# Four SSM states weighted by one GpSimd instruction, norm shifts on VectorE, and a new work order

## The reference

```
xn  = layernorm(x) * (1 + scale) + shift
u   = silu(conv(xn @ W_in));  dt = softplus(u @ W_x[:, :64] @ W_dt + b);  B, C = u @ W_x[:, 64:]
h_n(t) = h_n(t-1) * exp(dt(t) * A_n) + dt(t) * u(t) * B_n(t)       # per channel, all t in order
y(t)   = sum_n h_n(t) * C_n(t)
out = x + gate * ((y + u * D) * silu(z)) @ W_out
```

## Time and profile before

| | |
|---|---|
| median of 3 runs | 2023.14 us (2008.57 to 3804.73) |
| profiled execution | 2021.5 us, span 2019.3 us |
| busy: TensorE / VectorE / ScalarE / GpSimd | 1817.7 / 1780.9 / 1710.2 / 1789.5 us (90 / 88 / 85 / 89% of the span) |
| mean granted clock of TensorE | 0.961 |
| weightings on GpSimd (L969) | 510, 1197.2 us in all |
| scans on VectorE (L1581, L1578) | 576 + 448, 1198.5 us in all |
| DMA | 302.29 MB, mean 150 GB/s |

### The profile page before, as it was taken

The page is one execution under the profiler, slowest core; times in us unless marked ns, Lnnn a source line. Parts: engine busy times, 40 slices in busy tenths (PEclk is TensorE's granted clock), DMA queues, the critical chain, the costliest instruction groups (busy, mean ns, idle before and its releaser), DMA issues. The chain is left out here.

```text
span 2019.3 us, 29111 instructions
## 1 busy us (share of the span) xinstructions
PE 1817.7 (90%) x9252; PEld 1265.7 (63%) x9252; DVE 1780.9 (88%) x1818; ACT 1710.2 (85%) x3224; POOL 1789.5 (89%) x823
## 2 busy tenths in 40 slices
PE   8979688998989999998999999898998999697778
PEld 7555555757667575766667575656757575455666
DVE  5458999889999999999989999999989999898983
ACT  2488788989989999999989999999989998777662
POOL 0059999999999999999999999999999999999970
PEclk8989699999999999999999999999999999898999
DMA  7034554444445545454444545445444545454430
GB/s 279 1 110 156 169 165 149 139 159 155 150 140 171 167 146 181 130 182 153 146 150 152 178 149 175 147 157 162 157 140 155 166 154 180 142 162 142 155 105 11
DMA packets 163784, 302.29 MB, mean 150 GB/s; under 512 B 18904, under 2 KB 27312, under 8 KB 162096
## 3 DMA queue, kind: packets, MB, share of 16 engines
q1 hardware_dynamic: 153110, 287.45, 43.9%
q10 hardware_dynamic: 10522, 12.99, 2.1%
HBM read 292.98 MB, written 5.29 MB: 148 GB/s over the span
## 5 line engine op out<-in xcount | busy, mean ns | idle before, releaser
L969 POOL TENSOR_TENSOR state<-state,c_rows 128x1024 f32<-128x1024 f32 x510 | 1197.2, 2382 | 26.3 <-DVE state L1578 13.6
L1581 DVE TENSOR_TENSOR_SCAN state<-decay,mix_banks 128x512 f32<-128x512 f32 x576 | 673.1, 1206 | 15.7 <-ACT decay L1303 0.7
L2016 PE MATMUL bank<-const_sb,state 128*128 128x128 f32 x4096 | 546.4, 281 | 38.1 <-POOL state L969 37.7
L2016 PEld LDWEIGHTS bank<-const_sb,state 128*128 128x128 f32 x4096 | 482.1, 145 | 145.9 <-issue 76.4
L1578 DVE TENSOR_TENSOR_SCAN state<-mix_banks,state 128x512 f32<-128x512 f32 x448 | 525.4, 1204 | 48.0 <-ACT mix_banks L1284 36.4
L960 POOL TENSOR_TENSOR state<-kept,b_rows 128x1024 f32<-128x1024 f32 x224 | 532.4, 2381 | 19.7 <-DMA b_rows<-flat_rows 10.3
L1303 ACT ACTIVATE decay<-kept,ssm_pack 128x512 f32<-128x512 f32 x576 | 395.2, 716 | 17.0 <-DVE state L1581 14.2
L1571 DVE TENSOR_TENSOR mix_banks<-kept,mix_banks 128x1024 f32<-128x1024 f32 x288 | 353.5, 1227 | 42.4 <-ACT mix_banks L1292 33.6
L1284 ACT ACTIVATE mix_banks<-kept,ssm_pack 128x512 f32<-128x512 f32 x448 | 302.0, 683 | 57.4 <-DVE state L1581 42.2
L1836 PE MATMUL bank<-kept,conv_diag 128*128 128x512 f32 x496 | 225.3, 597 | 4.3 <-ACT kept L1224 3.8
L987 ACT ACT_TABLE_LOAD x165 | 211.7, 1283 | 8.8 <-issue 5.8
(11 more groups left out here) (206 smaller groups left out, 2237.9 us busy)
## 6 DMA issues: line engine op xcount, KB each, us to landing
b_rows<-flat_rows SPq DMA_DIRECT2D x512, 256.0 KB, 3.9
c_rows<-flat_rows SPq DMA_DIRECT2D x512, 256.0 KB, 3.6
conv_diag<-conv_diag SPq DMA_DIRECT2D x8, 1024.0 KB, 7.3
out<-x_res ACTq DMA_DIRECT2D x8, 512.0 KB, 3.2
ssm_pack<-ssm_pack SPq DMA_DIRECT2D x2, 1907.0 KB, 12.4
x_next<-x ACTq DMA_DIRECT2D x6, 512.0 KB, 6.7
x_again<-x_dbl ACTq DMA_DIRECT2D x16, 128.0 KB, 4.3
state<-ada_w SPq DMA_DIRECT2D x1, 1536.0 KB, 14.3
```

What stands on the lines that cost most here:

```text
L969: pool.tensor_tensor(st, st, by_pair(c_rows[:, row % ROWS]), ALU.mult).then_inc(m_prod, 1)
L1581: ins = dve.tensor_tensor_scan(st, decay[:, nth(g) % DECAYS], mixed, 0.0, ALU.mult, ALU.add)
L2016: ins = pe.matmul(y_banks[c2][:, t * P:(t + 1) * P], state[:, g % STATES, t * P:(t + 1) * P], ident, start=False, stop=(g == BANK_SUMS[g / ...
```

## The change

- **Weighting.** `weight` multiplies four states (two pairs, units g to g+3 with g a multiple of 4) by their two C rows in one GpSimd instruction over 128 x 2048, once both rows are loaded and scan g+3 is done. 510 instructions become 255. `m_prod` counts fours, so the sums, the C rows and ScalarE's `dtr` step wait for multiples of four. The two late pairs stay.
- **State slots.** 14 become 16 (a group of four always starts at a multiple of 4).
- **Shifts.** The 48 `shift` instructions move from GpSimd to VectorE, at the stages `root` and `yroot` of the tables, in front of `normed` where VectorE does the norm.
- **C rows.** SyncE issues C row g-3 behind B row g, where it was g-1, and the wait for a free C slot is rounded up to whole fours. At the end of a scan three C rows follow the last B row.
- **Order.** All the tables are new except the last attention's, which moves by a step in two places. Counted over the whole tables, in quarters of a unit: the weighting stands on average 6.0 behind the place of its last scan before and 3.7 after; the inject of a BESIDE pair stands 13.7 behind the sum that frees its slot before and 9.9 after; it leads its scan by 15.2 before and 17.3 after.

```diff
-BANKS, DECAYS, STATES, ROWS = 3, 7, 14, 4
+BANKS, DECAYS, STATES, ROWS = 3, 7, 16, 4
+WEIGHED = 4
...
-FIRST_BASES = {'att': (-53, -28), 'setup': -49, 'prep': -33}
-TAIL_BASE, POST_BASE, PREP_BASE = -19, -50, 8
-ATT_BASES, LATE_BASES = (18, 100, 153, 222), (41, 193)
+FIRST_BASES = {'att': (-53, -28), 'setup': -48, 'prep': -33}
+TAIL_BASE, POST_BASE, PREP_BASE = -17, -40, 9
+ATT_BASES, LATE_BASES = (17, 100, 152, 219), (51, 193)
...
+C_BEHIND = 3
...
-    "weight": (11, 7, 10, 5, 9, 8, 6, 8, 9, 14, 14, 11, 15, 13, 12, 8, 7, 8, 12, 7, 5, 8, 6, 12, 11, 19, 17, 14,
...
+    "weight": (25, 15, 16, 18, 16, 16, 15, 15, 17, 15, 13, 20, 19, 17, 17, 19, 15, 20, 13, 20, 19, 17, 17, 20, 19,
...
-    "weight": range(0, ALL_UNITS - HC * LATE_PAIRS, HC),
+    "weight": range(0, ALL_UNITS - HC * LATE_PAIRS, WEIGHED),
...
-                for g in range(HALVES * N + 1):
+                for g in range(HALVES * N + C_BEHIND):
...
-                    if g > 0:
-                        slot, n = (g - 1) % ROWS, (g - 1) % N
-                        past(sp, m_prod, si * HALVES * N + g - ROWS)
+                    if g >= C_BEHIND:
+                        g -= C_BEHIND
+                        slot, n = g % ROWS, g % N
+                        past(sp, m_prod, ((si * HALVES * N + g + 1 - ROWS) * HC + WEIGHED - 1) // WEIGHED)
...
-            def shift(norm, root, done, k):
-                pool.wait_ge(root, k)
-                pool.tensor_tensor(norm["shift"][:, :, 0], norm["minus"][:, :, 0], norm["rstd"][:, :, 0],
-                                   ALU.mult).then_inc(done, 1)
...
             def weight(g):
                 si, half, n, c2, c = split(g)
-                row = half * N + n
-                pool.wait_ge(c_loaded[row % ROWS], 16 * (si * (HALVES * N // ROWS) + row // ROWS + 1))
-                pool.wait_ge(m_scan, g + HC)
-                st = pair_states(g)
-                pool.tensor_tensor(st, st, by_pair(c_rows[:, row % ROWS]), ALU.mult).then_inc(m_prod, 1)
+                row, pairs = half * N + n, WEIGHED // HC
+                for k in range(row, row + pairs):
+                    pool.wait_ge(c_loaded[k % ROWS], 16 * (si * (HALVES * N // ROWS) + k // ROWS + 1))
+                pool.wait_ge(m_scan, g + WEIGHED)
+                st = state[:, g % STATES:g % STATES + WEIGHED, :].rearrange("p (n c) t -> p n c t", c=HC)
+                by_row = c_rows[:, row % ROWS:row % ROWS + pairs, :].unsqueeze(2).broadcast_to([P, pairs, HC, T])
+                pool.tensor_tensor(st, st, by_row, ALU.mult).then_inc(m_prod, 1)
...
-                past(act, m_prod, (pi - 1) * UNITS // HC)
+                past(act, m_prod, (pi - 1) * UNITS // WEIGHED)
...
+            def shift(norm, root, done, k):
+                dve.wait_ge(root, k)
+                dve.tensor_tensor(norm["shift"][:, :, 0], norm["minus"][:, :, 0], norm["rstd"][:, :, 0],
+                                  ALU.mult).then_inc(done, 1)
...
+                yield from w.to("root")
+                shift(att_norm, a_root, a_rstd, 2 * ai + 1)
                 yield from w.to("xn")
...
+                yield from w.to("yroot")
+                shift(att_norm, a_root, a_rstd, 2 * ai + 2)
+                if (ai, 1) in VECTOR_NORMS:
                     yield from w.to("yn")
...
+                yield from w.to("root")
+                shift(prep_norm, p_root, p_rstd, pi + 1)
+                if pi in VECTOR_PREPS:
                     yield from w.to("xn")
...
-                    pe.wait_ge(m_prod, g // HC + 1)
+                    pe.wait_ge(m_prod, g // WEIGHED + 1)
```

More of the change, by code:

```diff
@@ L198 @@
-    2: (199, 199, 210, 213, 215, 217, 219, 218, 218, 218, 224, 230, 231, 237, 240, 246, 251, 254, 257, 265, 269,
-        273, 276),
-    3: (216, 216, 218, 218, 219, 221, 222, 224, 224, 224, 226, 228, 230, 232, 237, 239, 245, 251, 253, 255, 258,
-        264, 266),
-    4: (201, 201, 206, 211, 216, 215, 217, 216, 216, 216, 218, 219, 219, 221, 228, 234, 237, 240, 240, 240, 240,
-        240, 240),
-    5: (213, 213, 216, 216, 218, 217, 221, 220, 220, 220, 224, 222, 227, 229, 234, 238, 240, 242, 242, 242, 242,
-        242, 242),
@@ L206 @@
-    6: (203, 203, 206, 210, 215, 220, 221, 222, 222, 222, 224, 227, 231, 233, 245, 251, 254, 261, 265, 268, 271,
-        274, 274),
-    7: (213, 213, 216, 216, 218, 219, 223, 222, 222, 222, 226, 225, 228, 230, 237, 240, 246, 253, 255, 260, 264,
-        267, 274),
-    8: (201, 201, 210, 213, 214, 215, 217, 216, 216, 216, 218, 218, 220, 222, 228, 234, 237, 240, 240, 240, 240,
-        240, 240),
-    9: (204, 204, 206, 212, 216, 217, 219, 218, 218, 218, 220, 219, 223, 225, 231, 236, 239, 246, 246, 246, 246,
-        246, 246),
@@ L214 @@
-    10: (201, 201, 206, 213, 218, 219, 225, 220, 220, 220, 231, 231, 236, 237, 243, 249, 253, 260, 265, 269, 270,
-         273, 276),
-    11: (215, 215, 218, 218, 220, 220, 224, 223, 223, 223, 225, 226, 227, 229, 236, 239, 243, 252, 254, 258, 264,
-         269, 272),
-    12: (200, 200, 202, 211, 214, 216, 217, 217, 217, 217, 218, 218, 219, 221, 227, 233, 237, 240, 240, 240, 240,
-         240, 240),
-    13: (204, 204, 210, 212, 213, 215, 216, 219, 219, 219, 220, 220, 222, 225, 230, 236, 238, 246, 246, 246, 246,
-         246, 246),
@@ L222 @@
-    14: (202, 202, 210, 211, 212, 215, 216, 218, 218, 218, 218, 218, 219, 220, 226, 229, 231, 230, 237, 239, 245,
-         252, 254),
-    15: (3, 3, 144, 144, 145, 147, 147, 154, 172, 206, 207, 207, 208, 210, 213, 213, 217, 214, 217, 221, 224, 224,
-         225),
+    0: (156, 156, 158, 159, 160, 173, 174, 180, 180, 180, 184, 182, 188, 190, 196, 199, 204, 206, 206, 206, 206,
+        206, 206),
+    1: (160, 160, 174, 176, 177, 178, 179, 179, 179, 179, 180, 181, 182, 185, 191, 197, 200, 206, 206, 206, 206,
+        206, 206),
@@ new lines @@
+    2: (173, 173, 176, 179, 180, 181, 191, 190, 190, 190, 194, 193, 196, 197, 200, 206, 212, 215, 221, 230, 234,
+        238, 242),
+    3: (180, 180, 182, 183, 184, 184, 186, 186, 186, 186, 188, 191, 195, 196, 199, 204, 210, 213, 229, 231, 234,
+        238, 242),
+    4: (167, 167, 174, 174, 175, 175, 176, 175, 175, 175, 177, 176, 178, 179, 184, 190, 196, 198, 198, 198, 198,
+        198, 198),
+    5: (164, 164, 170, 174, 176, 177, 177, 178, 178, 178, 178, 179, 179, 181, 190, 196, 198, 202, 202, 202, 202,
+        202, 202),
@@ new lines @@
+    6: (165, 165, 170, 176, 178, 181, 185, 186, 186, 186, 187, 188, 189, 192, 197, 199, 205, 211, 217, 222, 227,
+        231, 234),
+    7: (175, 175, 182, 183, 186, 185, 193, 189, 189, 189, 196, 195, 197, 198, 202, 208, 213, 215, 226, 230, 233,
+        238, 246),
+    8: (161, 161, 166, 173, 174, 175, 175, 175, 175, 175, 176, 177, 177, 179, 184, 190, 196, 198, 198, 198, 198,
+        198, 198),
+    9: (167, 167, 170, 174, 176, 177, 178, 178, 178, 178, 179, 181, 183, 185, 194, 197, 203, 206, 206, 206, 206,
+        206, 206),
@@ new lines @@
+    10: (170, 170, 174, 175, 180, 178, 187, 186, 186, 186, 190, 190, 192, 194, 198, 203, 208, 212, 218, 224, 229,
+         233, 238),
+    11: (174, 174, 177, 179, 179, 179, 186, 182, 182, 182, 188, 188, 192, 195, 199, 205, 210, 213, 219, 224, 228,
+         233, 238),
+    12: (165, 165, 170, 173, 174, 175, 175, 175, 175, 175, 176, 177, 177, 178, 183, 189, 196, 198, 198, 198, 198,
+         198, 198),
+    13: (164, 164, 166, 169, 173, 179, 181, 183, 183, 183, 184, 185, 188, 190, 196, 199, 204, 206, 206, 206, 206,
+         206, 206),
@@ L226 @@
+    14: (163, 163, 166, 172, 178, 181, 182, 183, 183, 183, 184, 184, 187, 189, 197, 201, 207, 206, 214, 217, 223,
+         228, 230),
+    15: (2, 2, 87, 96, 99, 100, 101, 110, 129, 166, 167, 167, 168, 170, 173, 173, 177, 174, 177, 181, 184, 184, 185),
 })
 TAIL_STAGES = by_name(TAIL_NAMES, {
-    0: (104, 105, 106, 106, 109),
-    1: (2, 68, 72, 73, 75),
-    2: (61, 75, 78, 86, 91),
-    3: (59, 73, 77, 85, 91),
-    4: (73, 88, 91, 93, 95),
-    5: (62, 75, 77, 79, 86),
-    6: (61, 75, 76, 79, 88),
@@ L235 @@
-    7: (61, 75, 77, 80, 92),
-    8: (74, 88, 89, 90, 94),
-    9: (63, 75, 77, 81, 89),
-    10: (62, 75, 77, 81, 90),
-    11: (62, 75, 76, 84, 91),
-    12: (69, 88, 90, 91, 94),
-    13: (62, 75, 76, 77, 89),
-    14: (56, 75, 80, 83, 89),
-    15: (59, 74, 77, 82, 87),
+    0: (94, 97, 98, 98, 103),
+    1: (3, 60, 64, 65, 67),
+    2: (50, 65, 66, 82, 85),
+    3: (50, 66, 70, 80, 86),
+    4: (68, 82, 85, 86, 90),
+    5: (63, 65, 67, 80, 82),
+    6: (61, 66, 67, 79, 83),
+    7: (51, 67, 72, 79, 85),
@@ L244 @@
+    8: (67, 81, 84, 85, 90),
+    9: (60, 66, 71, 77, 81),
+    10: (54, 68, 73, 78, 82),
+    11: (50, 66, 71, 77, 84),
+    12: (72, 81, 82, 83, 85),
+    13: (62, 66, 72, 78, 81),
+    14: (50, 67, 72, 75, 84),
+    15: (50, 66, 70, 83, 87),
 })
-SETUP_STAGES = dict(zip(SETUP_NAMES, (2, 47, 25, 51, 62, 96, 80, 84, 121, 147, 73, 168, 176, 179), strict=True))
+SETUP_STAGES = dict(zip(SETUP_NAMES, (0, 44, 22, 52, 74, 92, 77, 80, 117, 143, 69, 164, 172, 175), strict=True))
```

(30 more changed lines are left out.)

4 lines of the change are left out of this document (removed), and 414 rows, old and new, of tables (ATT_STAGES, PREP_STAGES, STEPS).

## The result

The changed kernel takes 2082.81 us (median of 4 runs, 2072.38 to 2086.02) against 2020.12 us for the kernel before: a ratio of 1.0321, 95% interval [1.0256, 1.0386]. It is 3.2% slower, where 1.5% faster was forecast. The ratio goes by the fast runs alone, so it leaves out a run of the kernel before of 3804.73 us. The profiled execution took 0.8 us less than its median (2081.98 us, span 2079.8 us).

A forecast was written before the change was run, and what follows sets the result against it. GpSimd, busy for 96.6% of the loop, was taken as the tightest engine, with VectorE next. The terms -36 - 6 - 8 + 1 + 18 = -31 us gave 1992 us against the median, range 1983 to 2005.

The forecast's parts named there:

- What one instruction of four states saves: GpSimd's weightings: one of 4.50 us replaces two of 2.32 us, 0.14 us saved for each of 255, 36 us.
- The price of a shift on VectorE: The 42 shifts in the loop: 0.18 us each on VectorE, 8 us, from a row before the loop.
- Which lie in VectorE's idle time of 1846.4 - 1704.2 = 142 us: VectorE in the loop: its idle time of 142 us covers the 8 us of shifts moved there.
- Rival 3: Loop's shifts on VectorE wait for GpSimd's instruction, 1.8 us on the mean; 2027 to 2145 us, centre 2040; chance 0.16.
- It decides from 1.7 us a shift on: VectorE in the loop: shift waits set the time once they reach 1.7 us each.
- Its counter-argument: VectorE's PSUM bank waits: a stall lets ScalarE fill banks, so part of it replaces 70 us of waits.
- The cited rule: VectorE instructions with two SBUF inputs and GpSimd ones reading SBUF contend; whichever starts second is blocked until the first ends.
- Slots, rows and order: GpSimd's waits before weightings and injects: thinner cushions add 18 us; C rows and slots 0, order 0 with 15 either way.
- The move off GpSimd: 42 shifts leaving GpSimd's queue in the loop: 6 us of work and 8 us of waits saved.
- Its signs of being wrong as a whole: The loop moving by more than 60 us either way, or the ends (111 and 62 us) by more than 3.

The follow-up runs named there:

- e2: Changed kernel with each shift on VectorE as four one-column instructions, rstd as scalar operand, so one SBUF tensor is read; 1994.23 us, ratio 0.9917.
- r5: Changed kernel with one-column shifts on VectorE and two states to a weighting instead of four; 1999.43 us, ratio 0.9938.
- e1: Changed kernel with the 48 shifts back on GpSimd at the same stages of the new tables; 2044.64 us, ratio 1.0166.
- r10: Kernel before with one-column shifts on VectorE and 16 state slots in place of 14, old tables and pairs; 2029.25 us, ratio 1.0079.
- e4: Kernel before with only the 48 shifts moved to VectorE, each as four one-column instructions; 2023.42 us, ratio 1.0061.
- r8: Changed kernel with one-column shifts on VectorE, each issued twice, once into a spare tile; 2015.56 us, ratio 1.0018.

## Why the prediction was wrong

- **What one instruction of four states saves: right.** 4.49 us from start to start (4.50), and 1742.8 us of GpSimd in the loop (1742). What it was worth is another matter: against pairs in the same tables, 4 us (e2 against r5).
- **The price of a shift on VectorE: the step that failed.** "For the forecast I take the low end, as it is the only row of this shape": 0.18 us, from a stretch in which GpSimd was idle. The loop has GpSimd busy for 91 to 97%, and there a shift took 107.0 / 42 = 2.55 us (all but the six outside, of 0.16 us each). The nearest row by shape was the farthest by condition.
- **"Which lie in VectorE's idle time of 1846.4 - 1704.2 = 142 us": wrong, and the larger error of method.** 81 us of stalls cost 81 us, 44 cost 46, and 23 us of plain work cost 20. Much of VectorE's idle time is made of short waits in front of scans and products for PSUM banks (70 us in all), and a stall elsewhere in its queue doesn't fill them; this reading fits the three doses but was not tested by itself. GpSimd, the busiest engine by share at 96.6%, did not set the time alone: 34 us less of its work brought 4, at the price of 26 us more of waits for scans.
- **Rival 3 is what happened, in mechanism and place; its sizes were short.** It gave 2040 as its centre and a chance of 0.16. It asked for 1.8 us of waiting on the mean, by a shift that comes at any time; a shift of 2.55 us was measured. Two things make the difference. 4 waits passed over further instructions. And shifts don't come at any time: of the 23 that began inside a weighting, 16 had more than 3.3 of its 4.5 us before them, 3.15 on the mean where 2.25 was put. From the measured 2.55 us its own sum makes (1704 + 107) / 0.966 = 1875 us of loop, and 1910.6 were measured: VectorE was busy for 1805.8 us, about as it says, but only for 94.5% of the loop. "It decides from 1.7 us a shift on" sets VectorE against GpSimd's old 1784 us; against the 1742 us that GpSimd would have left it is from (1742 - 1704) / 42 = 0.9 us on. The 65.5 us that ScalarE waited for the shift, and the chain behind it, had been left out; they are where to look for these 36 us, but no run shows them apart.
- **Its counter-argument did not hold.** "Part of the stall replaces the 70 us of waits for them": VectorE's waits for ScalarE did fall from 36.4 + 33.6 us to 29.5 + 13.5, but in e2, with the same tables and no stall, they are 30.0 + 12.3, and in e1, with the shifts on GpSimd, 71.8 + 25.3. The fall comes with the shifts' place on VectorE, not with their stalls.
- **The cited rule** (the Trainium skill, SBUF — State Buffer, "Who interferes with whom"): the trace agrees that a VectorE instruction with two SBUF tensors is held by GpSimd's: 37 of 37 long shifts end with a GpSimd instruction, and the one-tensor form never waits. "Until the first is through", as the prediction puts it, holds for 33 of the 37. That rule should have carried more than the absence of a row.
- **Slots, rows and order: +18 was near in size, not in kind.** In e2, free of the stalls, GpSimd waits 29.1 + 39.6 us before weightings and injects, 23 more than before, and nearly all of the wait before weightings is that for four scans (2.7 us with pairs, r5). In the changed kernel the two were 103.1 + 55.4 us, as the stalls came on top. r10 shows that the slots alone are worth nothing in the old tables, and the new tables, priced at 0 with 15 us either way, gave 25.
- **The move off GpSimd was no gain, where it was put at 6 + 8 us.** e4 takes 10 us of shifts off GpSimd, puts 27 us on VectorE and is 12 us slower than the kernel before.
- **Its signs of being wrong as a whole both came.** The loop moved by 64 us, over the 60, and the stretch before it by 4.1, over the 3. The second says little: with the same tables it was 107.7 us in e2 and 112.0 in r8.
